# A fused attention and FP4 feed-forward block on one Trainium2 core: one exponential per score bank, x requested ahead of a replication, residual loads and 704-column scales in other slots

## The reference

```python
h = _layernorm(x, axis=-1) * (1 + ca) + sa
x = x + ga * attention(h)        # 16 heads of 16 columns, scores + position_bias * 8, softmax, values, Wo
h = _layernorm(x, axis=-1) * (1 + cb) + sb
x = x + gb * ffn(h)              # h -> 704: silu(gate) * up; 704 -> 256: down
# in ffn the inputs and weights of each product are quantised to FP4 in blocks of 16:
scale = max(|block|) / 6;  q = grid[searchsorted(_MID, |block / scale|)] * sign * scale
```

## Time and profile before

| | |
|---|---|
| three runs | 3418.05, 3417.11, 3414.52 us (median 3417.11) |
| the profiled execution | 3417.14 us, its span 3415.2 us |
| mean granted TensorE clock | 0.979 |
| chain that ended last | PE 64%; issue 9%; DMA 8%; DVE 7%; SPq 5%; ACT 4% |
| twelve replication copies | k_rows 7.8 us, q_rows 4.7 us to landing (medians) |
| x into x_in, 512 KB | 8.7 us to landing (median) |

### The profile page before, as it was taken

The page is one execution under the profiler, slowest core; times in us unless marked ns, Lnnn a source line. Parts: engine busy times, 40 slices in busy tenths (PEclk is TensorE's granted clock), DMA queues, the critical chain, the costliest instruction groups (busy, mean ns, idle before and its releaser), DMA issues.

```text
span 3415.2 us, 81836 instructions
## 1 busy us (share of the span) xinstructions
PE 3166.1 (93%) x22404; PEld 1887.6 (55%) x22404; DVE 2832.6 (83%) x9960; ACT 2123.3 (62%) x3389; POOL 1720.2 (50%) x2104
## 2 busy tenths in 40 slices
PE   4899999999999999999999999999999999999985
PEld 1345555555555555555555555565555555555555
DVE  6678888888888888888888888888888888888855
ACT  2566666666666666666666666666666666666652
POOL 3425555554545544545554455554455545555455
PEclk7899999999999999999999999999999999999997
DMA  8344442433443433443333443332444242344000
GB/s 198 63 75 78 83 80 59 75 62 62 81 80 64 72 59 63 81 81 68 71 60 59 81 80 66 73 62 57 80 82 76 62 72 58 70 82 74 22 24 13
DMA packets 200320, 239.85 MB, mean 70 GB/s; under 512 B 23600, under 2 KB 178640, under 8 KB 199808
## 3 DMA queue, kind: packets, MB, share of 16 engines
q1 hardware_dynamic: 199840, 234.06, 36.6%
HBM read 164.57 MB, written 67.31 MB: 68 GB/s over the span
## 4 chain that ended last, share of the span: by engine, by line
PE 64%; issue 9%; DMA 8%; DVE 7%; SPq 5%; ACT 4%; DVEq 1%; POOL 0%; ACTq 0%; POOLq 0%
PE ps_x L681 20%; PE ps_o L670 10%; PE rings L652 10%; PE rings L635 9%; DMA x_in<-in_x 7%; PE ps_x L709 6%; SPq L521 5%; PE rings L638 3%; ACT probs L824 2%; PE ps_x L727 1%; DVE scale L1113 1%; DVE row_max L1078 1%; PE ps_x L716 1%; PE ps_x L733 1%; DVE x_mid L1196 1%
## 5 line engine op out<-in xcount | busy, mean ns | idle before, releaser
L1078 DVE CUSTOM_DVE_ANT_0 rings<-rings,band_z 128x512 f32<-128x512 f32 x2048 | 1415.7, 697 | 178.9 <-issue 172.3
L824 ACT ACTIVATE probs<-rings 128x1024 f32<-128x1024 f32 x1024 | 1047.7, 1023 | 583.3 <-PE rings L638 567.7
L652 PE MATMUL rings<-k_rows,q_rows 120*128 120x512 bf16 x2048 | 789.8, 387 | 108.5 <-DVE row_max L1078 106.5
L635 PE MATMUL rings<-q_rows,k_rows 121*128 121x512 bf16 x2048 | 704.9, 384 | 59.4 <-issue 27.3
L638 PEld LDWEIGHTS rings<-rev,band_t 128*128 128x128 f16 x5632 | 410.7, 98 | 292.7 <-issue 3.5
L670 PE MATMUL ps_o<-probs,values 128*32 128x512 f32 x4096 | 551.2, 610 | 0.0
L652 PEld LDWEIGHTS rings<-k_rows,q_rows 120*128 120x128 bf16 x2048 | 197.2, 96 | 585.6 <-DVE row_max L1078 463.8
L638 PE MATMUL rings<-rev,band_t 128*128 128x64 f16 x5632 | 501.6, 192 | 0.0
L681 PE MATMUL ps_x<-w_gu_h,xq_h 128*128 128x512 f32 (+1 forms) x768 | 356.7, 464 | 1.6 <-DVE xq_l L1123 1.6
L1366 POOL TENSOR_TENSOR ffn_in<-ffn_in,scale 128x256 f32<-128x256 f32 x128 | 79.5, 621 | 438.9 <-DVE ffn_in L1167 438.9
L681 PE MATMUL ps_x<-w_gu_h,xq_l 128*128 128x512 f32 (+1 forms) x768 | 288.9, 376 | 0.0
(11 more groups left out here) (180 smaller groups left out, 6666.5 us busy)
## 6 DMA issues: line engine op xcount, KB each, us to landing
parts_dram<-parts SPq DMA_DIRECT2D x128, 384.0 KB, 2.3
q_rows<-parts_dram SPq DMA_DIRECT2D x384, 128.0 KB, 4.7
k_rows<-parts_dram SPq DMA_DIRECT2D x384, 128.0 KB, 7.8
mod_rows<-mod_rows_dram SPq DMA_DIRECT2D x32, 640.0 KB, 6.9
x_in<-in_x SPq DMA_DIRECT2D x32, 512.0 KB, 8.7
x_mid<-in_x SPq DMA_DIRECT2D x128, 128.0 KB, 2.1
out<-x_mid SPq DMA_DIRECT2D x128, 128.0 KB, 1.7
k_rows<-band_dram SPq DMA_DIRECT2D x2, 1024.0 KB, 9.4
```

The source lines that it names most:

```text
L635: mm(ps_s[:, bank, :], kr[0:ROW_MAX + 1, h, k0:k0 + P], qr[0:ROW_MAX + 1, h, :], start=True, stop=False)
L652: mm(ps_m[:, bank, :], q_rows[par][0:ROW_MAX, h, j * P:(j + 1) * P], k_rows[par][0:ROW_MAX, h, :], start=True, stop=True).then_inc(mscores ...
L824: A(prob_pair(s, j), ps_s, ACT.Exp).then_inc(exp_done, 1)
L1078: v.tensor_tensor_reduce(ps, ps, band_z[:, bias:bias + S], 1.0, LOWEST, ALU.add, ALU.max, row_max[:, par, 4 * h + j:4 * h + j + 1]).then_i ...
```

## The change

1. PE computes one score product at every position, and ACT takes one exponential of 512 columns for each bank; `exp_done` counts 64 per batch, not 32.
2. The scales of 704 columns on DVE move from (2,2) to (3,0), POOL's multiplication by the inverse from r = 2 to r = 3, ACT's square from (3,1) to (3,3), ahead of the identity. The statistics of x lie at (2,3), (3,1), (3,2), (3,3).
3. `load_x` in slot 0 stands ahead of the replication of heads 8 to 15, which moves from the end of an iteration to slot 0 of the next.
4. The out stores move from slots 3, 7, 11, 15 to 5, 9, 13 and 1 of the next iteration; the loads into `x_mid` from slots 0, 4, 8, 12 to 3, 7, 11, 15.

```diff
-LN1_STATS = ((2, 3), (3, 0), (3, 1), (3, 3))
+LN1_STATS = ((2, 3), (3, 1), (3, 2), (3, 3))
...
         @block.sync
...
-            def replicate(it, half):
-
-
-                wait(sp, scores_ready, 64 * it.n + 32 * (half + 1))
-                for op, dst in ((0, q_rows[it.par]), (1, k_rows[it.par])):
-                    wait(sp, parts_stored[2 * half + op], 16 * (it.n + 3))
-                    src = parts_dram[it.par, half, op].rearrange("(h d) c n -> c d h n", d=HD)
+            def replicate(it, half, back):
+
+                n, par = it.n - back, (it.par + back) % 2
+
+                wait(sp, scores_ready, 64 * n + 32 * (half + 1))
+                for op, dst in ((0, q_rows[par]), (1, k_rows[par])):
+                    wait(sp, parts_stored[2 * half + op], 16 * it.n + 16 * (3 - back))
+                    src = parts_dram[par, half, op].rearrange("(h d) c n -> c d h n", d=HD)
...
                     if s == 11 and it.has(2):
-                        replicate(it, 0)
+                        replicate(it, 0, 0)
                     if s == 0 and it.has(2) and (it.steady or n > FIRST + 1):
                         load_x(n + 2)
+                    if s == 0 and it.has(1):
+                        replicate(it, 1, 1)
...
-                    if s % 4 == 0 and it.has_tile(s, -1):
-
-                        t = s // 4
-                        wait(sp, stored[t], 16 * (n - 1))
-                        sp.dma_start(x_mid[:, t, :], x_v[:, bass.ds(n - 1, 1), t, :].rearrange("p b d -> p (b d)")
-                                     ).then_inc(xres_loaded[t], 16)
...
-                    if s % 4 == 3 and it.has_tile(s, 2):
-                        after(sp, f3_dve, it.tile(s, 2), "out")
-                        tt = (s // 4 + NT - 3) % NT
-                        sp.dma_start(out_v[:, bass.ds(it.tile(s, 2), 1), :].rearrange("p b d -> p (b d)"),
-                                     x_mid[:, tt, :]).then_inc(stored[tt], 16)
-                if it.has(2):
-                    replicate(it, 1)
...
+                    if s % 4 == 1 and it.has_tile(s, 3):
+                        after(sp, f3_dve, it.tile(s, 3), "out")
+                        sp.dma_start(out_v[:, bass.ds(it.tile(s, 3), 1), :].rearrange("p b d -> p (b d)"),
+                                     x_mid[:, s // 4, :]).then_inc(stored[s // 4], 16)
+                    if s % 4 == 3 and it.has_tile(s, -1):
+
+                        t = s // 4
+                        wait(sp, stored[t], 16 * (n - 1))
+                        sp.dma_start(x_mid[:, t, :], x_v[:, bass.ds(n - 1, 1), t, :].rearrange("p b d -> p (b d)")
+                                     ).then_inc(xres_loaded[t], 16)
...
         @block.tensor
...
-                if bank == 0:
-                    wait(pe, exp_done, it.n * 32 + 2 * s + j // 2)
+                wait(pe, exp_done, it.n * 64 + 4 * s + j - 1)
...
-                wait(pe, exp_done, prev * 32 + 2 * (u + 1))
+                wait(pe, exp_done, prev * 64 + 4 * (u + 1))
...
                         if j == 1:
                             weigh(it, s)
-                        if j % 2 == 0 and it.has(0):
+                        if it.has(0):
                             scores(it, s, j)
-                            scores(it, s, j + 1)
                         maxima(it, s, j)
...
         @block.scalar
...
-                        if j % 2 == 0 and it.has(0):
-                            wait(act, scores_ready, n * 64 + (4 * s + j) + 2)
+                        if it.has(0):
+                            wait(act, scores_ready, n * 64 + (4 * s + j) + 1)
...
-                            A(prob_pair(s, j), ps_s, ACT.Exp).then_inc(exp_done, 1)
+                            A(prob(s, j), ps_s[:, j % RING_S, :], ACT.Exp).then_inc(exp_done, 1)
...
-                        if (r, j) == (3, 1) and it.has_tile(s, 1):
+                        if (r, j) == (3, 3) and it.has_tile(s, 1):
                             u = it.tile(s, 1)
                             after(act, f2_pool, u, "xn")
                             after(act, f3_pool, u - 1, "sub")
                             A(magic3[:], hidden[:, g % 2, :], ACT.Square, scale=ROOT).then_inc(f3_act.sem, 1)
-                        if (r, j) == (3, 3) and it.has_tile(s, 1):
-                            after(act, f3_act, it.tile(s, 1), "sq")
+                            after(act, f3_act, u, "sq")
                             A(magic3[:], magic3[:], ACT.Identity, bias=floor[:]).then_inc(f3_act.sem, 1)
...
         @block.vector
...
-                            if at == (2, 2):
+                            if at == (3, 0):
                                 after(dve, f2_dve, u, "h2")
                                 after(dve, f3_pool, u - 1, "q")
                                 block_scales(f2_dve, u, scale3[:], inv3[:], hid)
...
         @block.gpsimd
...
-                    if r == 2 and it.has_tile(s, 1):
+                    if r == 3 and it.has_tile(s, 1):
                         hid = hidden[:, g % 2, :]
                         after(pool, f2_dve, it.tile(s, 1), "inv")
```

More of the change, by code:

```diff
@@ L430, in prob @@
             return probs[:, 2 * (unit % 2) + j if j < 2 else 2 + j, :]
-        def prob_pair(unit, j):
-            at = 2 * (unit % 2) if j < 2 else 4
-            return probs[:, at:at + 2, :]
         def gate_up(w, kt, op, n0):
@@ L536, in emit @@
                     if s == 11 and it.has(2):
-                        replicate(it, 0)
+                        replicate(it, 0, 0)
                     if s == 0 and it.has(2) and (it.steady or n > FIRST + 1):
                         load_x(n + 2)
+                    if s == 0 and it.has(1):
+                        replicate(it, 1, 1)
+                    if s == 0 and not it.steady and n == FIRST + 1:
+                        place_consts()
                     if s == 8 and not it.steady and n == FIRST:
@@ L557, in emit @@
                                 "p h (b q) -> p (h b) q", q=P), max_rows[:]).then_inc(max_placed[half], 16)
-                    if s % 4 == 3 and it.has_tile(s, 2):
-                        after(sp, f3_dve, it.tile(s, 2), "out")
-                        tt = (s // 4 + NT - 3) % NT
-                        sp.dma_start(out_v[:, bass.ds(it.tile(s, 2), 1), :].rearrange("p b d -> p (b d)"),
-                                     x_mid[:, tt, :]).then_inc(stored[tt], 16)
-                if it.has(2):
-                    replicate(it, 1)
-                if not it.steady and it.n == FIRST:
-                    place_consts()
+                    if s % 4 == 1 and it.has_tile(s, 3):
[7 more added lines that the diff above has]
+                                     ).then_inc(xres_loaded[t], 16)
             iterations(sp, emit)
```

## The result

The changed kernel took **3596.55 us** (median of 4 runs, 3593.12 to 3599.22) against 3415.82 us for the kernel before (4 runs, 3411.27 to 3418.05): a ratio of **1.053**, 95% interval 1.0512 to 1.0549. It is 181 us slower, where 99 were forecast, and lies above the range. The profiled execution took 3593.12 us (span 3591.3) at a mean granted clock of 0.958; before it was 0.979.

A forecast was written before the change was run, and what follows sets the result against it. TensorE, 93% busy, was taken as the bound. Per iteration +5.1 (late load, scales' 1.49 included) - 1.2 (x) - 0.39 (exponentials) = +3.5 us; 3417.1 + 102 (29 iterations) - 3 = 3516 us, range 3400 to 3555.

The forecast's parts named there:

- The late load: Slot 11's x_mid load, queued behind twelve copies: issued about 1584.4, landing 1594.1, making POOL's reader 9.4 us late.
- Rival B: The slot 11 load lands quickly despite the copies, leaving only gains: 3325 us, or 3371 with half; chance 0.17.
- Part (4): Moved out stores and x_mid loads: slot 11's load delays PE in slot 14, +5.1 us at the iteration's end.
- rival D: Worse: PE's 4 to 5 us idle lowers its clock, or ACT's extra times add up; over 3550 us, chance 0.06.
- inside* the delay of ACT: DVE's own wait for POOL's late reader, 4.4 us, was taken as covered by PE's 5.6 us lateness in slot 14.
- The gains: Better order on PE returns 3.08 us per iteration: 1.49 from scales, 1.2 from x, 0.39 from exponentials.
- I take the gain, 0.39 us per iteration: Single exponentials per bank: PE's 10.6 us of waits on exponentials all go, with ACT's extra time costed at 0.
- With today's times this just fits: Fourth exponential behind ACT's normalisation ends at 1597.7, before PE's weighting product at 1598.04: 0.3 us of slack.
- The 1.49 us goes, 1.49 us per iteration: Moving the 704-column scales to slot 3 removes PE's wait for a row maximum in slots 14 and 15.
- The 27.3 us of issue: PE's issue waits over 27 iterations, 12 pieces, once per loop of two iterations; not counted among recoverable time.
- x requested ahead: SP requests x 17 us earlier, before the replication; DVE's wait goes, returning 1.2 us of PE per iteration.
- starts up to 5 us earlier, when the last scores are there; nobody waits for it before slot 10: Replication of heads 8 to 15, moved past x, was taken as harmless, with no cost in the sum.

## Why the prediction was wrong

**The late load: right in place and cause.** Issued behind the copies at the moment of its reader, landed 9.5 us later, forecast 9.7 (1584.4 to 1594.1). The Trainium skill ("DMA: Bandwidth & Descriptors", anatomy of one DMA) fits a DMA that GpSimd issues as about 2 us plus its bytes at 436 GB/s; by that, as an estimate, the load would be there in under 4 us. The trace of these DMAs, issued by SP, disagrees: from 1546 to 1558 us its windows of 3 us show 127 to 262 GB/s at DMA shares of 1.10 to 1.16. L836 starts 10.1 us behind the weighting product of slot 13 on the mean, where it starts 4.4 behind it with the load ahead: 5.7 us late, forecast 5.9. Rival B falls.

**Its price: nearly right, partly by luck.** Part (4) said +5.1 us with the 1.49 us of the old gap in it, 6.6 alone; measured 6.0 in the changed kernel. But it was summed as idle time only. By the waits, the changed kernel stands 130.2 / 24.5 = 5.3 us per iteration on maxima, with the load ahead 47.5 / 26.1 = 1.8, so 3.5 us are idle; PE's busy time is 58 us higher (3260.2 against 3202.1), 2.0 us per iteration, for the same order of products at a clock of 0.958 instead of 0.974; the rest is mostly the longer issue gap. The clock stood only in rival D, at 0.06: that the 6.6 came so near is luck in so far as a third of the loss is clock, which the sum didn't hold. And the way ran through DVE's L1140, which I had put *inside* the delay of ACT.

**The gains: the step that failed.** The sum took off 3.08 us per iteration, 92 us; with the load put right none of it is there (3422.33 against 3417.07). The 3.08 is itself a little low: it divides by 27 iterations, and the window holds 26.1, which gives 3.19. Term by term:

- "I take the gain, 0.39 us per iteration" for the exponentials: alone on the kernel before they cost 75 us, 2.5 per iteration. The text named what is not free, the fourth exponential behind L843, and then priced it at 0, since "With today's times this just fits". It looked at slot 13 alone, and at the weighting product; the one who comes late is DVE, behind the tanh that now stands behind both. 40 us came back when L836 and the copies of slots 9 and 13 were put behind the exponential.
- "The 1.49 us goes, 1.49 us per iteration" for the scales: slot 15 gains it in every second iteration. In the other the loop's jump follows, and takes it back: PE waits there until 1.9 us after a packet that comes no sooner than before, and more often at a lower clock. The 27.3 us of issue were read and then left as a constant.
- x requested ahead: DVE's wait for it is gone, and slot 3 takes 5.5 us where it took 6.9 and 7.6, 1.8 us less on the mean, more than the 1.2 us forecast. What stood beside it, "starts up to 5 us earlier, when the last scores are there; nobody waits for it before slot 10", of the replication of heads 8 to 15, failed: with x ahead of it, it fills the DMA engines while PE jumps back, which costs 20 to 27 us.

So the sum should have read: 29 x 6.0 = 174 for the load, and about +5 instead of -92 for everything else, which gives 3596. The sign was right because the load's price is twice what the rest could have returned.

**Open:** what sets the start of the packet that the jump waits for, some 5.2 us behind the weighting product of slot 15 with quiet DMA engines. Of the 20 to 27 us, gap and clock were read apart (4.5 and 21.6 us with the load ahead; 1.2 us of gap at each of 12 jumps, 15 us, and 14 us of busy time with the load late), but no run moved one without the other. Why the clock fell after some gaps of 2 or 3 us and not after others isn't known either.

## What to carry to other kernels

A small load that is needed soon goes into a queue *ahead* of a bulk transfer: one line's difference was worth 166 us here. When an engine's step is cut in two and the second half lands behind an instruction that waits for another engine, look at everything queued behind it on that engine, in every slot in which that happens, before costing the order at nothing. And an idle of PE of several us can cost more than its length, since the granted clock was lower after most of them: count busy time of PE as well as waits when two versions are compared, and remember that an order of products changes it too. Last, time won just ahead of a hardware loop's jump need not be won: here it was spent waiting for the jump.

## What the runs showed of the hardware

- The gap in PE's issue at a hardware loop's jump back isn't constant: on the mean 2.3 us before, 2.9 with the load ahead and the requests later (DMA share 0.03), 3.3 with the load ahead alone (0.50 to 0.76), 4.1 in the changed kernel (0.64 to 1.01), 5.6 in the changed kernel with pairs (1.1 in the windows read); but also 3.3 at 0.03 where only the scales moved. At 151 jumps PE's first score came 1.7 to 2.5 us after the end of a 16 KB packet of the queue that the profile calls instruction.
- The granted clock over the 5 us that follow such a gap was 0.69 and 0.66 (gaps of 3.04 and 3.16 us, load ahead) and 0.71 (4.59 us, changed kernel), but 1.00 after 2.15 us in the kernel before and after 2.85 and 3.18 us with quiet DMA engines. In the kernel before it was 0.66 behind 7 of 12 jumps, one of them after a gap of 1.85 us.
- A 128 KB load behind twelve copies of 128 KB landed 9.5 us after its issue; one line ahead of them, no reader waited for it.
- PE's busy time for the same 22404 instructions rose by 26 us at the same clock (0.978 against 0.979) when score products were issued one by one and not in pairs.
